# Joining the first experts' block with the block that combines them and projects, and reordering the work inside

## The reference, cut to what matters

```python
x = x + jnp.tanh(g_ffn[0]) * _L0_ffn_ref(_layernorm(x, axis=-1), ...)      # each token: 2 of 8 experts, weighted
x = x + jnp.tanh(g_xattn[1]) * _L1_xattn_ref(_layernorm(x, axis=-1), ctx_2048, w_qkv, w_proj, b_proj)
# in _L1_xattn_ref: q, k, v = x @ w_qkv.T ; keys and values of the context stand before those of x
```

## Time and profile before

| | before |
|---|---|
| median of 3 runs | 1381.57 us (1381.45 to 1382.24) |
| the profiled execution | 1377.27 us |
| its span, first to last instruction | 1375.5 us |
| mean granted TensorE clock | 0.897 |
| busy share of the span: PE, DVE, ACT, POOL | 83%, 55%, 43%, 25% |

### The profile page before, as it was taken

How to read it: one execution, slowest core, us unless ns; L and a number is a source line. 1 busy time by engine, 2 the same in 40 slices (tenths; PEclk the granted TensorE clock), 3 DMA queues, 4 the chain that set the end, 5 groups by cost and what they waited for, 6 DMA issues and landing times. The chain is left out here.

```text
span 1375.5 us, 27252 instructions
## 1 busy us (share of the span) xinstructions
PE 1136.9 (83%) x6984; PEld 744.3 (54%) x6986; DVE 756.3 (55%) x2072; ACT 587.3 (43%) x1394; POOL 337.3 (25%) x538
## 2 busy tenths in 40 slices
PE   4849999999947789999999999997548999999300
PEld 2749999999944422333333233324417888888200
DVE  6552222222236387888788888832694555555533
ACT  2631222122224406777777777785353333333000
POOL 2012222222111353111111101010004333333476
PEclk9959999999977958999999999999658999999755
DMA  5455554555432622303203123042107888888444
GB/s 169 135 198 185 188 185 168 184 187 184 152 102 85 121 79 35 47 4 50 39 12 49 24 26 48 1 128 70 49 0 231 250 254 250 253 249 253 128 131 118
DMA packets 139940, 172.73 MB, mean 126 GB/s; under 512 B 17574, under 2 KB 118944, under 8 KB 139738
## 3 DMA queue, kind: packets, MB, share of 16 engines
q1 hardware_dynamic: 126186, 138.75, 36.3%
q0 software_dynamic: 11376, 31.08, 8.0%
q10 hardware_dynamic: 2304, 2.10, 0.4%
HBM read 141.29 MB, written 30.38 MB: 125 GB/s over the span
## 5 line engine op out<-in xcount | busy, mean ns | idle before, releaser
L1940 DVE TENSOR_REDUCE arena<-ps 128x1 f32<-128x512 f32 x512 | 327.7, 682 | 66.6 <-PE ps L1781 59.7
L1911 ACT ACTIVATE arena<-ps 128x512 f32<-128x512 f32 (+1 forms) x576 | 304.0, 598 | 135.7 <-PE ps L1822 134.2
L1822 PE MATMUL ps<-arena 99*128 99x512 bf16 (+1 forms) x576 | 216.7, 389 | 6.1 <-ACT arena L1911 5.7
L1781 PE MATMUL ps<-arena 96*128 96x512 bf16 x512 | 206.0, 405 | 8.8 <-PEq L1349 6.1
L896 POOL DMA_INDIRECT xg<-xn,tcol x134 | 127.7, 953 | 341.2 <-DVE tcol L929 338.9
L1811 PE MATMUL ps<-arena 128*17 128x512 f32 (+1 forms) x1152 | 153.3, 604 | 2.1 <-ACT arena L1911 1.0
L1822 PEld LDWEIGHTS ps<-arena 99*128 99x128 bf16 (+1 forms) x576 | 57.1, 101 | 179.4 <-ACT arena L1911 139.6
L1145 PE MATMUL ps<-scratch,arena 128*128 128x128 f32 x1140 | 147.8, 280 | 5.6 <-DMA arena<-in_L_ffn_w 2.6
L987 PEld LDWEIGHTS ps<-scratch,arena 128*128 128x128 f32 x1248 | 147.8, 195 | 3.6 <-issue 1.7
L987 PE MATMUL ps<-scratch,arena 128*128 128x128 f32 x1248 | 148.3, 278 | 1.1 <-ACT scratch L1018 1.1
L1145 PEld LDWEIGHTS ps<-scratch,arena 128*128 128x128 f32 x1140 | 135.9, 193 | 12.9 <-issue 9.0
(11 more groups left out here) (306 smaller groups left out, 1263.7 us busy)
## 6 DMA issues: line engine op xcount, KB each, us to landing
arena<-in_L_ffn_W SPq DMA_DIRECT2D x47, 1024.0 KB, 4.9
arena<-in_L_ffn_w SPq DMA_DIRECT2D x190, 192.0 KB, 3.6
y<-ysb SPq DMA_DIRECT2D x95, 128.0 KB, 4.0
arena<-k_parts SPq DMA_DIRECT2D x48, 137.6 KB, 4.9
arena<-q_parts SPq DMA_DIRECT2D x96, 64.0 KB, 5.5
arena<-y SPq DMA_DIRECT2D x16, 256.0 KB, 5.4
arena<-in_L_ffn_w SPq DMA_DIRECT2D x8, 512.0 KB, 8.3
xg<-xn,tcol POOLq DMA_INDIRECT x134, 4.4
```

Of the source, the lines that this page charges most:

```text
L1781: nc.tensor.matmul(ps[:, MAXB + pos % NMAXB, :], e.q_aug[u][0:QROWS, c, h, t * P:(t + 1) * P], e.k_aug[u][0:QROWS, h, CL + k * HB:CL + (k ...
L1822: nc.tensor.matmul(ps[0:rows, SB + n % NSB, :], e.k_aug[u][0:AROWS, h, k0:k0 + rows], e.q_aug[u][0:AROWS, c, h, :], start=True, stop=True) ...
L1911: nc.scalar.activation(e.prob[s % 2][0:rows, h, :], ps[0:rows, SB + (s * GH + h) % NSB, :], ACT.Exp).then_inc(p_ready, 1)
L1940: v.tensor_reduce(e.mx[:, c, h, t, k:k + 1], ps[:, MAXB + pos % NMAXB, :], AX.X, ALU.max).then_inc(max_done, 1)
```

## The change

It does six things.

1. `combine_and_project` no longer opens a block: it returns one program per engine, and the experts' block runs each behind the experts' own on the same engine. The barrier and the drains between the two are gone.
2. SyncE, no longer GpSimd, waits for the last scatter (`y_stored`), ahead of the 16 loads of `y`. TensorE's context transposes wait for the last tile of the experts (`y_ready`).
3. The clearing of semaphores with its second barrier stands between the routing and the experts' block.
4. The context goes first: its parts and differences come before `combined(0)` and `norm(0)`.
5. `combined(c+2)` is split: two tiles, `left(c,0)`, one tile, `left(c,1)`, one tile with the variance, `left(c,2)`, `left(c,3)`, then the shift, then `values(c+1)`. ScalarE: `first_parts(c)`, root(c+2), `second_parts(c)`, norm(c+2), copy(c+2). TensorE: V(c), `turn(c+1)`, U(c) for every c.
6. The memset of L1353 goes to the attention's GpSimd program, beside L1733, each with its wait.

```diff
 def experts0_and_project(e):
+    project = combine_and_project(e, y_ready, y_stored)
     with nc.Block() as block:
-        move_tiles(e, 0, block, gathered, tcol_ready, y_ready, y_stored)
+        @block.gpsimd
+        def _(pool):
+            move_tiles0(e, pool, gathered, tcol_ready, y_ready, y_stored)
+            project.gpsimd(pool)
...
             tile_loop(sp, NT0, RING0, body)
+            project.sync(sp)
...
+    def sync(sp):
+        sp.wait_ge(y_stored, 16 * NT0)
+        y = e.y[0][0:NTOK * kk, :].rearrange("(k i p) d -> p i k d", k=kk, p=P)
+        for i in range(NTILE):
+            sp.dma_start(yg[:, i, :, :], y[:, i, :, :]).then_inc(got[i], 16)
...
+        pe.wait_ge(w_done, len(wturn))
+        pe.wait_ge(y_ready, NT0)
...
+        turn(0)
+        for c in range(CH):
...
+            if c + 1 < CH:
+                turn(c + 1)
...
+        first_parts(-1, CL)
+        second_parts(-1, CL)
+        for c in range(2):
+            root(c)
+            norm(c)
+            copy(c)
+        for c in range(CH):
+            first_parts(c, HB)
+            if c + 2 < CH:
+                root(c + 2)
+            second_parts(c, HB)
+            if c + 2 < CH:
+                norm(c + 2)
+                copy(c + 2)
...
+        for n in range(4):
+            left(-1, n, CL)
+        for c in range(2):
+            i = c * CHUNK
+            combined(c, (i, i + 1))
+            combined(c, (i + 2, i + 3))
+            shifts(c)
+        values(0)
+        for c in range(CH):
+            i = (c + 2) * CHUNK
+            if c + 2 < CH:
+                combined(c + 2, (i, i + 1))
+            left(c, 0, HB)
+            if c + 2 < CH:
+                combined(c + 2, (i + 2,))
+            left(c, 1, HB)
+            if c + 2 < CH:
+                combined(c + 2, (i + 3,))
+            left(c, 2, HB)
+            left(c, 3, HB)
+            if c + 2 < CH:
+                shifts(c + 2)
+            if c + 1 < CH:
+                values(c + 1)
...
-            g_.memset(e.k_aug[1][QROWS:AROWS, :, :], 1.0).then_inc(ones_set, 1)
-            pool.wait_ge(ones_set, 1)
+            for u in range(2):
+                g_.memset(e.k_aug[u][QROWS:AROWS, :, :], 1.0).then_inc(ones_set, 1)
+                pool.wait_ge(ones_set, u + 1)
...
-        for stage, *args in ((prepare,), (mix_and_score,), (route, 0), (experts0,)):
+        for stage, *args in ((prepare,), (mix_and_score,), (route, 0)):
             stage(e, *args)
         nc.clear_and_free_semaphores(e.used)
         nc.all_engine_barrier()
         e.used = []
-        for stage, *args in ((combine_and_project,), (attend,), (project_and_score,), (route, 1), (experts1,), (combine1,)):
+        for stage, *args in ((experts0_and_project,), (attend,), (project_and_score,), (route, 1), (experts1,), (combine1,)):
             stage(e, *args)
```

More of the change, by code:

```diff
@@ L882, in _, with move_tiles0, gather, scatter @@
             nc.tensor.transpose(ps[0:1, 2, 0:P], first, e.ident[:]).then_inc(first_raw, 1)
-def move_tiles(e, layer, block, gathered, tcol_ready, y_ready=None, y_stored=None):
-    nt, ring = ((NT0, RING0), (NT1, RING1))[layer]
-    carrier = e.sem(f"ga{layer}_carrier")
+def move_tiles0(e, pool, gathered, tcol_ready, y_ready, y_stored):
+    nt, ring = NT0, RING0
+    carrier = e.sem("ga0_carrier")
     LAG = 2 + ring
+    def gather(j, r):
+        pool.wait_ge(tcol_ready, j + 1)
+        pool.sem_inc(carrier, 1)
+        pool.indirect_dma_start(out=e.xg[:, r, :], out_offset=None, in_=e.xn[0],
+                                in_offset=bass.IndirectOffsetOnAxis(ap=e.tcol[:, r:r + 1], axis=0)).then_inc(gathered[r], 16)
+    def scatter(j, r):
+        if isinstance(j, int) and j < 0:
+            return
+        pool.wait_ge(y_ready, j + 1)
+        pool.sem_inc(carrier, 1)
+        if not (isinstance(j, int) and j == 0):
+            pool.wait_ge(y_stored, j * 16)
+            pool.sem_inc(carrier, 1)
+        pool.indirect_dma_start(out=e.y[0], out_offset=bass.IndirectOffsetOnAxis(ap=e.rcol[:, r:r + 1], axis=0),
+                                in_=e.ysb[:, r, :], in_offset=None).then_inc(y_stored, 16)
+    head = LAG + 1 + ring - (LAG + 1) % ring
+    for j in range(head):
+        gather(j, j % ring)
+        scatter(j - LAG, (j - LAG) % ring)
+    turns = (nt - head) // ring
+    with pool.Fori(0, turns) as t:
+        for u in range(ring):
+            gather(t * ring + (head + u), u)
+            scatter(t * ring + (head + u - LAG), (u - LAG) % ring)
+    for j in range(head + turns * ring, nt + LAG):
+        if j < nt:
+            gather(j, j % ring)
+        scatter(j - LAG, (j - LAG) % ring)
+def gather_tiles1(e, block, gathered, tcol_ready):
+    nt, ring = NT1, RING1
+    carrier = e.sem("ga1_carrier")
     @block.gpsimd
@@ L895, in gather, with experts0_and_project @@
             pool.sem_inc(carrier, 1)
-            pool.indirect_dma_start(out=e.xg[:, r, :], out_offset=None, in_=e.xn[layer],
+            pool.indirect_dma_start(out=e.xg[:, r, :], out_offset=None, in_=e.xn[1],
                                     in_offset=bass.IndirectOffsetOnAxis(ap=e.tcol[:, r:r + 1], axis=0)).then_inc(gathered[r], 16)
[L899 to L914, removed]
+        for j in range(ring):
+            gather(j, j)
+        turns = (nt - ring) // ring
         with pool.Fori(0, turns) as t:
             for u in range(ring):
[L917 to L924, removed]
+                gather(t * ring + (ring + u), u)
+        for j in range(ring + turns * ring, nt):
+            gather(j, j % ring)
 def token_column(e, dve, j, r, ready):
     e.nc.vector.tensor_copy(e.tcol[:, r:r + 1], e.token_u[:, bass.ds(j, 1)]).then_inc(ready, 1)
-def experts0(e):
+def experts0_and_project(e):
     nc, ps, sem = e.nc, e.ps, e.sem
@@ L1346, in combine_and_project @@
     NTR = 4
[L1349 to L1353, removed]
-            pool.wait_ge(ones_set, 1)
-            def third_parts(c, w):
-                for n in range(4):
[L1359 to L1370, removed]
-            for n in range(4):
[L1372 to L1388, removed]
-            for n in range(4):
[L1390 to L1450, removed]
-                    nc.scalar.activation(e.parts[c % 2][:, n, 0, 0:w], ps[:, UB + n, 0:w], ACT.Copy, scale=SCALE[n // DK] if c >= 0 else 1.0).then_inc(part0, 1)
-            def second_parts(c, w):
-                for n in range(4):
-                    act.wait_ge(left1, (c + 1) * 4 + n + 1)
-                    nc.scalar.activation(e.parts[c % 2][:, n, 1, 0:w], e.left[:, n, 0:w], ACT.Copy).then_inc(part1, 1)
[L1458 to L1463, removed]
-            for c in range(CH):
-                if c + 2 < CH:
-                    norm(c + 2)
-                first_parts(c, HB)
-                if c + 2 < CH:
-                    copy(c + 2)
-                second_parts(c, HB)
-        @block.vector
-        def _(dve):
-            v = nc.vector
-            ch = Chain(dve, step)
-            for b in range(B):
-                v.tensor_copy(e.v_all[0:CL, b, 0, :], e.ctx[:, b, D:2 * D])
-            v.tensor_scalar(e.bproj, e.bproj, e.tg[:, 1:2], None, ALU.mult)
-            def combined(c):
-                for pair in (c * CHUNK, c * CHUNK + 2):
-                    for i in (pair, pair + 1):
-                        dve.wait_ge(got[i], 16)
-                        v.scalar_tensor_tensor(e.x[:, i, :], yg[:, i, 0, :], e.gate[:, i, 0:1], e.x[:, i, :], ALU.mult, ALU.add).then_inc(summed, 1)
-                    for i in (pair, pair + 1):
-                        dve.wait_ge(summed, i + 1)
-                        v.scalar_tensor_tensor(e.x[:, i, :], yg[:, i, 1, :], e.gate[:, i, 1:2], e.x[:, i, :], ALU.mult, ALU.add).then_inc(added, 1)
-                    for i in (pair, pair + 1):
-                        dve.wait_ge(added, i + 1)
-                        ins = v.bn_stats(e.stats[:, i, :], e.x[:, i, :])
@@ new lines, in vector, with combined @@
+    def vector(dve):
+        v = nc.vector
+        ch = Chain(dve, step)
+        for b in range(B):
+            v.tensor_copy(e.v_all[0:CL, b, 0, :], e.ctx[:, b, D:2 * D])
+        v.tensor_scalar(e.bproj, e.bproj, e.tg[:, 1:2], None, ALU.mult)
+        def combined(c, tiles):
+            for i in tiles:
+                dve.wait_ge(got[i], 16)
+                v.scalar_tensor_tensor(e.x[:, i, :], yg[:, i, 0, :], e.gate[:, i, 0:1], e.x[:, i, :], ALU.mult, ALU.add).then_inc(summed, 1)
+            for i in tiles:
+                dve.wait_ge(summed, i + 1)
+                v.scalar_tensor_tensor(e.x[:, i, :], yg[:, i, 1, :], e.gate[:, i, 1:2], e.x[:, i, :], ALU.mult, ALU.add).then_inc(added, 1)
+            for i in tiles:
+                dve.wait_ge(added, i + 1)
+                ins = v.bn_stats(e.stats[:, i, :], e.x[:, i, :])
+            if i % CHUNK == CHUNK - 1:
@@ new lines, in left, with values @@
+        def left(c, n, w):
+            dve.wait_ge(part0, (c + 1) * 4 + n + 1)
+            if c >= 0:
```

(8 more changed lines are left out.)

115 lines of the change are left out of this document (86 added, 29 removed).

## The result

The changed kernel took 1366.19 us in the median of 4 runs (1365.19 to 1368.12), against 1381.51 (4 runs, 1379.78 to 1382.24) of the kernel before: a ratio of 0.989 (95% interval 0.9875 to 0.991). The profiled execution took 1365.19 us with a span of 1362.9, 12.6 shorter than before. In a later job on another chip the same pair gave 1368.55 and 1379.02, ratio 0.991 (0.988 to 0.994). The forecast of 1366.0 was met, and part of that is luck: two of its steps were wrong in opposite directions.

The account below looks back on a forecast made before the run. The prediction took a chain of waits between 400 and 425 us, with no engine full, to bound that stretch. Gains of 7.7 + 4.5 + 3.3 = 15.5 us from 1381.6 gave 1366.0 us, range 1361 to 1373.

Parts of the forecast that it names:

- The gap: From the last `ysb` written (390.7) past GpSimd's drain, clearing and barrier to VectorE's first sums of `y` at 406.09.
- The drain: GpSimd's 6.45 us at the old block's end: taken as unfinished DMA time, holding nobody else once the blocks are joined.
- 7.85 and 8.1: Microseconds from the last indirect DMA's end to the drain's end, at another block's end and at the experts' block's end.
- the drain comes back: Rival: the drain's 6.45 us recur at the new block's end; gain 9.1, 1372.5 us; chance 0.09.
- The loads: Loads of `y` after the last scatter: sums start at 398.4 instead of 406.09, worth 7.7 us (7.0 to 8.4).
- The clearing and barrier: At the old boundary: their 1.1 us move ahead of the experts, not saved, delaying everything up to the last scatter.
- Context first: First sum to U(0): VectorE's idle 4.19 and the context's differences 0.67 go, TensorE next late; 4.5 us (4.2 to 5.2).
- Interleaving: U(0) to U(2): two steps take 28.0 us (26.4 without contention) instead of 31.3; gain 3.3 us (0.3 to 4.9).
- The moved memset: At the attention's start: 3.8 + 0.3 us more fit into GpSimd's idle time; without that cover it would cost 4.1.
- The sum: Whole projection: gains of 7.7, 4.5 and 3.3 us add to 15.5, carried unchanged from U(2) to the end.

Follow-up runs that it names:

- experiment 2: Changed kernel plus a GpSimd drain behind the context's third parts, with further drains in the experts' loop, per DMA pair or per eight: 1361.87 and 1363.23 us.
- e8_memset_moved: The kernel before with only its memset moved from the projection's block to the attention's: 1381.17 us, ratio 1.001.

## Why the prediction was right or wrong

*What bounds it: right.* The gap and the chain behind it were pure waiting: all of the 19.3 us taken from them by U(2) are still there at GpSimd's last third part.

*The drain: wrong.* The step that failed is "GpSimd being unfinished for some 8 us after such a DMA; nobody else need wait". From 7.85 and 8.1 I took it for time since the last DMA. What the runs showed in its place is work that the drain itself does, some 0.08 us for each indirect DMA since the last drain, 6.5 us here, whenever the drain comes. By it the two numbers are different things. The 8.1 are 1.45 us until GpSimd left its wait for the landing, and the drain of 78 DMAs behind it; the 7.85 are the drain of 95 gathers, with no such wait ahead of it (7.9 by the line of experiment 2). That they agree to 0.25 us is chance, and in the other traces the 7.85 is up to 8.8. I took the one agreement as evidence. The rival "the drain comes back" had 0.09 and happened: 6.5 us on the path.

*The loads: right,* 7.9 for 7.7. The clearing and barrier cost 0.9 at the experts' start (the first token columns at 97.5 instead of 96.5) and 0.6 at the stage's end, for 1.1. That VectorE's copies might hold up the scatter's descriptors (the Trainium skill, "SBUF — State Buffer", section "SBUF: two separate sides", the box on the trap) did not show, and had no occasion to: the copies end at 391.7, before the scatter starts at 392.18; it takes 0.97 us as before.

*Context first: right in kind, too small.* 6.7 us instead of 4.5. VectorE's wait went, and TensorE was next late, as worked out; but V(0) took 5.00 us, not 7.2. The clock rose within it (columns as in the earlier trace rows), which I had priced at "up to 1 us less"; it was 2.2. That size is not fixed: V(0) took 4.91 to 6.15 us in the other traces with the context first.

```profile
410.00:411.00 1.00, 1.00 (x5) 0.83 (x5) 0.49 (x3) 0.94 (x2) 0.00 (x0) 0.83 0.36 26
```

*Interleaving: right in kind, too small.* The two steps from U(0) to U(2) took 26.6 us, the number of the rows without contention (26.4), not 28.0. A single tile took 1.37, estimated 1.5. Contention did appear where the Trainium skill's page "SBUF — State Buffer", section "Who interferes with whom", has it (an operation of VectorE with two SBUF inputs beside one of GpSimd that reads SBUF): the shift's last operation, with two SBUF inputs, took 0.88 us instead of 0.16 beside a third part, in both steps; the first pair of sums 1.18 instead of 0.87. Part of the 0.7 us reached the path. The second step, with the shift on VectorE, the third tile of V(2) on TensorE and ScalarE's first copy behind it:

```profile
435.80 0.88 DVE L500 SCALAR_TENSOR_TENSOR shift<-ln_tmp,rstd 128x4 f32<-128x4 f32 x1
437.16 1.97 PE L1431 MATMUL ps<-arena 128*128 128x256 f32 x8 [1.25 <-DVE arena L1531]
439.38 0.66 ACT L1462 ACTIVATE arena<-ps 128x256 f32<-128x256 f32 x2 [0.43 <-PE ps L1420]
```

The third tile waits for a value copy that stands behind the shift, so a shift of 0.16 would bring it and the transposes forward by 0.7. ScalarE's copy could come 0.43 earlier, as ScalarE's norm ends then. That is an estimate of 0.4 us a step on the path, where the term took 0.8 and its bound was 2.3. So the agreement with 26.4 is luck in part: without contention the step would be about 12.9 us, not 13.2, for which the shorter single tiles are one reason.

*The moved memset: right,* free at the attention; in the old block it gained nothing either (`e8_memset_moved`).

*The sum.* Forecast gain at U(2) 15.5, measured 19.3; less the drain's 6.5, 12.9. The two errors, 3.8 too little and 6.5 too much, left 2.6 in the trace; the medians of the first job happened to differ by 15.3, those of the second by 10.5.

## What to carry to other kernels

A drain of GpSimd behind indirect DMAs has work of its own, which grows with their number and falls to the first drain that comes; a block's end is one, so put a drain where GpSimd has nothing to do (6 us here for one line). When two blocks are joined, ask of each cost at the old boundary whether it goes with the boundary or waits at the next one. An order that opens a new wait where it stands alone (context first in two blocks, which gave 1.7 us of its gain back) can be worth more once another change has put a wait there anyway, in which that one is hidden.

## What the runs showed of the hardware

- GpSimd's drain ended 6.5 us after its last work with 78 indirect DMAs since the last drain, 1.1 with 12, 5.3 with 64 and 7.8 to 8.8 with 95, and a drain behind every pair of them (28 in all) cost the stage nothing. Its ordinary element-wise work ran 2.2 us after a scatter without paying any of it.
- An operation of VectorE on 128 x 4 elements with two SBUF inputs took 0.88 us instead of 0.16 beside GpSimd's third parts; the reciprocal ahead of it, with one SBUF input, took its usual 0.17.
- The same attention code took 457.5 to 465.6 us in different executions, with a later rise or dips of the granted clock in the longer ones that were followed.
